# Routed experts in two bf16 halves: weights split during the dense attention, loaded once per expert, picked by a register on TensorE

## The chip, the cores and the metric

One core of a Trainium2 chip runs the whole program. The metric is device time in microseconds (us), the median of the runs shown. TensorE is PE in the profile, its weight loads PEld, VectorE is DVE, ScalarE ACT, GpSimd POOL, and SyncE (which only issues DMAs here) SP.

## The reference

Four layers in a row, each added to `x` (4 x 256 tokens of width 256):

```
x = x + cross_attention(layernorm(x), ctx_2048, ...)   # 16 heads, 4 kv heads, 1601 + 256 keys
x = x + moe(layernorm(x), ...)                         # 32 experts, top 6, plus a shared expert
x = x + window_attention(layernorm(x), ctx_2048, ...)  # 9 keys for each query
x = x + ffn(layernorm(x), ...)                         # weights rounded to e4m3
# moe, for each chosen expert e of a token (H = 256, M = 176):
out = silu(x @ w_gate[e]) * (x @ w_up[e]) @ w_down[e]  # summed over 6 experts with their gates
```

All inputs and the output are float32.

## The kernel before

**The dense attention** (`attend`) takes two thirds of the time. It runs 16 groups (4 batches x 4 kv heads) of 8 tiles of 128 query rows; a tile's turn is a slot, so a job "at (g, i)" is done in slot i of group g. In a slot PE computes the scores of the next tile (L542), turns the probabilities of the last one in four quads (L551) and multiplies them by V in two bf16 halves (L565). ACT copies each turned quad to the high bf16 half (L729) and takes the exponentials (L735); DVE makes the low half (L920) and the row maxima (L907); POOL rotates the keys of the next group. Each engine works through its own list strictly in order.

In some slots an operand in float32 is split into bf16 halves on the side: a job of `JOBS_AT` (L123). SP loads it into one of two `stage` buffers (`split_load`, L337), ACT makes the high half (`split_high`, L757) at a fixed place of its slot, ahead of its third quad copy, DVE makes the low half (`split_low`) at the end of the slot (in slot 6 ahead of the tasks in its middle), and SP stores weights to HBM (`split_store`, L344). Before the change there are 20 jobs: 12 in groups 0 to 2, and context pieces in slots 2 and 6 of groups 5, 6, 9 and 10.

SP's own list orders the DMAs. For each group from 3 on it waits for PE's last output projection of the group before, which runs in slot 1, loads `wo` (L394), stores the rows for the window layer (`near_store`), loads two small tables (L355), and only then comes to the jobs of this group. For job j it first issues the loads up to job j + 1, then the store of j:

```python
for j in [j for j, (at, _) in enumerate(JOBS_AT) if at[0] == g]:
    while ahead < len(SPLITS) and ahead <= j + 1:
        split_load(ahead)
        ahead += 1
    split_store(j)
```

**The experts** (`experts`) come after routing. Tokens are sorted by expert into 80 tiles of 128 rows (NSLOT). There are 96 jobs in one software pipeline: 16 of the shared expert, then 80 routed ones. In step j PE does `gate_up(j)` (L1520), turns the rows of tile j + 2 (`turn_rows`, L1508), does `down(j - 2)` (L1537 and L1538) and turns the hidden values of j - 1 (`turn_hidden`, L1527). All products are float32. ACT does SiLU (L1569), copies the turned rows (L1574) and the result (L1579); DVE multiplies gate and up (L1654) and copies the turned hidden values (L1659). POOL gathers the rows of each tile with an indirect DMA 11 tiles ahead (L1459) and scatters its result with another (L1464). SP loads the weights of each tile's expert (480 and 48 KB, L1433 and L1434) into a ring of eight, with the expert's number read into a register. On the side DVE rounds the last layer's weights to e4m3 (`quantize`, L1686 to L1696): 32 parts of 144 columns, ten operations each, each waiting for the one before, in every second step; and `shares` (L1673 to L1675) takes three operations in each of six steps. After the last scatter SP loads the results back (L1448) and DVE and PE add them to `x`.

Of the kernel before, what the change touches and what calls it, by code (L numbers as in the profile page):

```python
# [15 lines left out]
P = 128  # L16
# [37 lines left out]

FI = 768
# [103 lines left out]
def attend(nc, t, x, groups=GROUPS):  # L159
# [4 lines left out]
    with Scope(nc, "att") as sc:  # L164
# [31 lines left out]
        stage = sc.sb("stage", [P, 2, 1024])  # L196
# [16 lines left out]
        spare = prob[:, :, :]  # L213
        start_from = {("wkv", 0): attn[:, 0:4, :].rearrange("p m d -> p (m d)"), ("wkv", 1): attn[:, 4:8, :].rearrange("p m d -> p (m d)"),
# [12 lines left out]
                 "sums_ready", "mean_done", "mean_ready", "mean_out"]  # L227
# [47 lines left out]
        def split_from(job):  # L275
            kind = job[0]
            return {"wkv": lambda h: t["wkv_l"][:, 512 * h:512 * h + 512], "wq": lambda h: t["wq_l"][:, 1024 * h:1024 * h + 1024],
                    "wo": lambda h: t["wo_l"][:, 1024 * h:1024 * h + 1024],
                    "ctx": lambda b, q: t["ctx_l"][b][:, :, CHUNKS[q][0] * P:(CHUNKS[q][0] + CHUNKS[q][1]) * P]}[kind](*job[1:])

        def staged(job, home):
# [4 lines left out]
            return home[:, 0:512 if job[0] == "wkv" else 1024]  # L286

        def split_to(job, a):

            if job[0] == "ctx":  # L290
                k0, m = CHUNKS[job[2]]
                return kvT[:, job[1] % 2, a, :, S + k0 * P:S + (k0 + m) * P]
            par = job[1] % 2
# [11 lines left out]
        def tokens(b):  # L305

            home = cosd[:, :, :] if b == 0 else flat[:, 1, 0:2 * D].rearrange("p (m d) -> p m d", d=HD)
            return home
# [6 lines left out]
        with nc.Block() as block:  # L315
            @block.sync
            def _(sp):
# [26 lines left out]
                def split_store(j):  # L344
# [3 lines left out]
                    sp.wait_ge(s["split_lo"], j + 1)  # L348
                    dst, src = store_of(job)
# [35 lines left out]
                for g in range(groups):  # L385
# [17 lines left out]
                    if g == 2:  # L403
# [4 lines left out]
                        sp.wait_ge(s["late_stored"], 16 * sum(job[0] != "ctx" and job not in (("wo", 0), ("wo", 1)) for job in SPLITS))  # L408
# [272 lines left out]
            def _(act):  # L681
# [75 lines left out]
                def split_high(j):  # L757
                    job = SPLITS[j]
                    act.wait_ge(stage_in[j % 2], 16 * (j // 2 + 1))
                    if job[0] == "ctx":  # L760

                        wait(act, s["nk_done"], NCH * (job[1] - 1))
                    elif job[0] == "wo":
# [104 lines left out]
            def _(dve):  # L868
# [82 lines left out]
                def normalise(b):  # L951
                    dve.wait_ge(s["rstd_ready"], b + 1)
                    for n in range(2):
# [36 lines left out]
                def extra(i, g):  # L990

                    b, at = g // KVH, (g % KVH, i)
                    if b + 1 < B:
                        if at == STATS_AT:
                            token_stats(b + 1)
                        if at == NORMALISE_AT:
                            normalise(b + 1)
                        for k in TRIG_AT.get(at, ()):
                            trig_step(b + 1, k)
# [1248 lines left out]
```

## Time and profile before

| | us |
|---|---|
| median of 3 runs (1864.81 to 1865.66) | 1865.14 |
| the profiled execution's own time | 1864.89 |
| its span, first to last instruction | 1862.8 |
| PE busy | 1710.4 (92%) |
| DVE, ACT, POOL busy | 1405.2, 1103.7, 1100.0 |

The span's stages: start and first group to 58, full groups of the dense attention to 1183, its last group to 1257, normalisation and routing to 1293, shared expert to 1344, routed experts to 1585, adding up, window attention and last layer to 1863. "Busy" counts an engine's own instructions; the last part of a row, in brackets or behind the bar, is the idle time ahead of the instruction and what ended it.

### The profile page before, as it was taken

Reading aid. Unit: us, or ns where it says so; the run is one execution under the profiler, and the core shown is the slowest. Engines: PE = TensorE matmul, PEld = TensorE weight load, DVE = VectorE, ACT = ScalarE, POOL = GpSimd, SP = SyncE. Lnnn points to the kernel's source line nnn. Section 1 sums busy time; section 2 is a strip of 40 time slices with the busy share of each in tenths; the row PEclk is TensorE's granted clock in tenths of the full one; section 3 lists DMA queues with packets and bytes.
Section 4 is the critical chain, followed back from the end, with each engine's and each line's share of the span. In section 5 each row is a group of like instructions: output and inputs, shape, how many; then the busy total and the mean of one; then the engine's idle time right before and its main releaser. Section 6 shows DMA issues by size and latency. Waiting matters only on the chain. (4 is left out here: it accounts for less than half of the span.)

```text
span 1862.8 us, 41598 instructions
## 1 busy us (share of the span) xinstructions
PE 1710.4 (92%) x14581; PEld 1314.5 (71%) x14727; DVE 1405.2 (75%) x3734; ACT 1103.7 (59%) x2798; POOL 1100.0 (59%) x1718
## 2 busy tenths in 40 slices
PE   4799999999999999999999999986999999589987
PEld 3578777788787787877787887765555555339974
DVE  7898886888877878888788788756656665575746
ACT  6576777676777667777676666652134333173534
POOL 5578695786866958868568577510266664181210
PEclk8899999999999999999999999996999999796998
DMA  3211111011010100110001000325389996500100
GB/s 126 75 52 30 61 39 50 19 36 47 18 39 19 37 20 18 59 32 19 19 19 36 24 1 24 122 92 220 101 253 269 275 267 188 189 15 24 43 9 26
DMA packets 69529, 140.24 MB, mean 75 GB/s; under 512 B 10921, under 2 KB 38674, under 8 KB 69074
## 3 DMA queue, kind: packets, MB, share of 16 engines
q1 hardware_dynamic: 58514, 105.37, 18.3%
q0 software_dynamic: 9984, 30.42, 4.8%
q8 instruction: 120, 1.97, 0.4%
q10 hardware_dynamic: 832, 1.84, 0.3%
q14 instruction: 79, 0.65, 0.1%
HBM read 111.73 MB, written 25.86 MB: 74 GB/s over the span
## 5 line engine op out<-in xcount | busy, mean ns | idle before, releaser
L920 DVE TENSOR_TENSOR att_pT<-att_pT 128x512 bf16<-128x512 f32 (+1 forms) x512 | 320.9, 650 | 166.2 <-ACT att_pT L729 163.1
L565 PE MATMUL att_out<-att_V,att_pT 128*128 128x128 bf16 x5760 | 386.8, 219 | 13.9 <-DVE att_pT L920 12.0
L565 PEld LDWEIGHTS att_out<-att_V,att_pT 128*128 128x128 bf16 x5760 | 349.0, 98 | 40.8 <-DVE att_pT L920 24.3
L729 ACT ACTIVATE att_pT<-att_pT 128x512 bf16<-128x512 f32 (+1 forms) x512 | 278.0, 572 | 128.8 <-PE att_pT L551 128.8
L735 ACT ACTIVATE att_prob<-att_scores,att_negmax 128x512 f32<-128x512 f32 (+1 forms) x512 | 330.3, 655 | 17.5 <-DVE att_negmax L909 16.9
L542 PE MATMUL att_scores<-att_K,att_Q 128*128 128x512 bf16 (+1 forms) x1408 | 298.5, 359 | 7.2 <-DVE att_Q L881 0.5
L907 DVE TENSOR_REDUCE att_mx<-att_scores 128x1 f32<-128x512 f32 (+1 forms) x512 | 291.0, 629 | 1.0 <-PE att_scores L542 0.9
L551 PE MATMUL att_pT<-att_ident,att_prob 128*128 128x128 f32 x1920 | 274.2, 274 | 0.0
L542 PEld LDWEIGHTS att_scores<-att_K,att_Q 128*128 128x128 bf16 x1536 | 150.6, 98 | 144.1 <-issue 1.9
L551 PEld LDWEIGHTS att_pT<-att_ident,att_prob 128*128 128x128 f32 x1920 | 208.6, 141 | 0.8
L465 PE MATMUL att_aux<-att_wkv,att_kvT 128*128 128x256 bf16 x1350 | 167.2, 273 | 17.8 <-DVE att_aT L881 15.2
L653 POOL TENSOR_TENSOR att_scaled<-att_kvraw,att_kw 128x256 f32<-128x256 f32 (+1 forms) x123 | 89.9, 731 | 135.7 <-ACT att_kvraw L697 135.7
L465 PEld LDWEIGHTS att_aux<-att_wkv,att_kvT 128*128 128x128 bf16 x1350 | 127.9, 98 | 35.6 <-DVE att_aT L881 18.8
L655 POOL TENSOR_TENSOR att_cosd<-att_scaled,att_tab 128x256 f32<-128x256 f32 (+2 forms) x153 | 127.2, 831 | 12.0
L1464 POOL DMA_INDIRECT y_s<-moe_ysb,moe_result_row x80 | 79.6, 995 | 76.2 <-ACT moe_ysb L1579 76.2
L667 POOL TENSOR_TENSOR att_rs<-att_rs,att_nhalf 128x2 f32<-128x2 f32 (+2 forms) x153 | 122.5, 801 | 0.0
L1459 POOL DMA_INDIRECT moe_xg<-xrow_s,moe_token_row x80 | 77.8, 972 | 60.4 <-DVE moe_token_row L1643 36.1
L1569 ACT ACTIVATE moe_silu<-moe_up 128x176 f32<-128x176 f32 x96 | 30.5, 318 | 136.0 <-PE moe_up L1520 136.0
L735 ACT ACTIVATION_READ_ACCUMULATOR att_prob<-att_scores,att_negmax 128x1 f32 x512 | 109.5, 214 | 0.0
L1520 PE MATMUL moe_up<-moe_wa,moe_xT 128*128 128x352 f32 x320 | 107.9, 460 | 0.0
L697 ACT ACTIVATE att_kvraw<-att_aux 128x512 f32<-128x512 f32 x120 | 68.7, 572 | 40.4 <-PE att_aux L465 40.1
L662 POOL TENSOR_TENSOR att_rs<-att_kss,att_eps 128x2 f32<-128x2 f32 (+1 forms) x123 | 30.6, 248 | 96.9 <-DVE att_kp L891 96.9
(347 smaller groups left out, 3250.6 us busy)
## 6 DMA issues: line engine op xcount, KB each, us to landing
moe_wa<-in_wa_l SPq DMA_DIRECT2D x80, 480.0 KB
att_wq<-wq_s SPq DMA_DIRECT2D x12, 512.0 KB, 3.7
att_wo<-wo_s SPq DMA_DIRECT2D x12, 512.0 KB, 3.8
att_stage<-in_ctx_l SPq DMA_DIRECT2D x9, 512.0 KB, 4.3
near_s<-att_windows POOLq DMA_DIRECT2D x8, 576.0 KB, 5.5
win_near<-near_s SPq DMA_DIRECT2D x32, 144.0 KB
moe_wb<-in_wb_l SPq DMA_DIRECT2D x80, 48.0 KB
moe_wa<-y_s SPq DMA_DIRECT2D x5, 768.0 KB, 11.0
```

Source lines behind the costliest of these rows:

```text
L465: last = nc.tensor.matmul(o, kvT[:, bp, a, c, k0:k0 + P], wkv[:, par, w, c, :], start=(c, a, w) == (0, 0, 0), stop=(c, a) == (DC - 1, 1))
L542: last = nc.tensor.matmul(scores[:, lo:lo + n], Q[:, u, a, i, :], K[:, u, w, lo:lo + n], start=(a, w) == (0, 0), stop=a == 1)
L551: last = nc.tensor.transpose(pT_ps[j % 2][:, m, :], prob[:, i % 2, k0:k0 + P], ident[:, :])
L565: last = nc.tensor.matmul(out_ps[:, i % 2, :], pT[:, i % 2, a, k, :], V[:, par, k, w, :], start=(k, a, w) == (0, 0, 0), stop=(k, a) == (KT ...
L653: eng.tensor_tensor(a, raw_[:, 0:m, :], weight[:, :].unsqueeze(1).to_broadcast([P, m, HD]), ALU.mult).then_inc(linked, 1)
L655: eng.tensor_tensor(b.rearrange("p m (e f) -> p m e f", e=2), a.rearrange("p m (e f) -> p m e f", e=2), cos.unsqueeze(2).to_broadcast([P, ...
L667: eng.tensor_tensor(scale, scale, nhalf[:, 0:m], ALU.pow).then_inc(linked, 1)
L729: nc.scalar.activation(pT[:, i % 2, 0, 4 * j:4 * j + m, :], pT_ps[j % 2][:, 0:m, :], ACT.Copy).then_inc(s["pt_hi"], 1)
L735: nc.scalar.activation(prob[:, i % 2, lo:lo + n], scores[:, lo:lo + n], ACT.Exp, bias=negmax[:, i % 4:i % 4 + 1], scale=1.0, accum_out=es[ ...
L907: nc.vector.reduce_max(mx[:, i % 2, k:k + 1], scores[:, lo:lo + n], AX.X).then_inc(s["bank_max"], 1)
L920: nc.vector.tensor_tensor(pT[:, i % 2, 1, 4 * j:4 * j + m, :], pT_ps[j % 2][:, 0:m, :], pT[:, i % 2, 0, 4 * j:4 * j + m, :], ALU.subtract) ...
L1520: last = nc.tensor.matmul(up_ps[j % 2][:, 0:GU], rows, w[:, c * GU:(c + 1) * GU], start=c == 0, stop=c == DC - 1)
```

## The change

- The 32 experts' weights are laid out as one array of [32, 128, 1056] float32. 32 more split jobs, `("we", e)`, run in groups 3 to 14 of the dense attention: in slots 0, 2, 6 and 7 of groups 3, 7, 11, 12, 13 and 14, in slots 2 and 6 of groups 4 and 8, in slots 0 and 7 of groups 5 and 9. Both halves go to one buffer in the `windows` tile and from there to HBM by two DMAs; a job's `split_high` waits until the stores of all earlier expert jobs have landed (`expert_out`).
- SP loads the bf16 halves of each expert once, in order of the experts, into a ring of eight, with constant addresses; a place is used again when all tiles of its expert are through. It reports arrivals in order with the semaphore `have`.
- PE reads the tile's expert number into a register, waits for `have`, and addresses the ring with it. Each float32 product becomes three bf16 ones (high x high, high x low, low x high): 6 matmuls of 352 columns for gate and up, 6 of 256 columns for down. The transposes stay float32, and so does the shared expert.
- ACT makes the high half of turned rows and hidden values, DVE the low half from PSUM: two operations on DVE and two on ACT per tile where there was one each.
- `quantize` works on 8 parts of 576 columns and issues one operation in each of the 80 routed steps. `begun_of` (when each expert's tiles begin) is one small DVE operation more. The results come back into `y6` and `w8` (6 places where there were 7).
- `tokens(b)` moves to the other half of `windows`; POOL waits for the expert stores in the last group.

```diff
+SPLIT_E, SPLIT_W = 32, 1056
+EXPERT_AT = [(g, i) for g in range(3, GROUPS - 1) for i in ((0, 2, 6, 7) if g % KVH == 3 or g > 12 or g == 12 else ((2, 6), (0, 7), ())[g % KVH])]
+JOBS_AT = sorted(JOBS_AT + [(at, ("we", e)) for e, at in enumerate(EXPERT_AT)], key=lambda x: x[0])
...
+                    if job[0] == "we":
+                        sp.dma_start(t["wu_s"][job[1]], halves_out[:, :, 0:DC * GU]).then_inc(s["expert_out"], 16)
+                        sp.dma_start(t["wd_s"][job[1]].rearrange("a (p n) -> p a n", p=P), halves_out[:, :, DC * GU:SPLIT_W]).then_inc(s["expert_out"], 16)
+                        return
...
+                    elif job[0] == "we":
+                        wait(act, s["expert_out"], 32 * job[1])
...
-        PARTS = NSLOT * 2 // 5
+        PARTS = NSLOT // QUANT_STEPS
...
+                def fetch(e):
+
+                    u = e % WRING
+                    sp.dma_start(wu[:, u, :, :], t["wu_s"][e]).then_inc(load[u], 16)
+                    sp.dma_start(wd[:, u, :, :], t["wd_s"][e][:, 0:P * D].rearrange("a (p n) -> p a n", p=P)).then_inc(load[u], 16)
+                    sp.dma_start(we[:, u, :, :], t["wd_s"][e][:, P * D:M * D].rearrange("a (p n) -> p a n", p=REST)).then_inc(load[u], 16)
...
+                for e in range(E_ALL):
+                    if e == WRING:
+                        sp.wait_ge(s["begun_of"], 1)
+                    if e >= WRING:
+
+                        begun = sp.value_load(begun_of[0:1, e - WRING + 1:e - WRING + 2], min_val=0, max_val=NSLOT)
+                        sp.wait_ge(s["y_done"], begun + SHARED)
+                    fetch(e)
+                    if e >= BEHIND:
+                        report(e - BEHIND)
...
+                        e = pe.value_load(expert_of[0:1, i:i + 1], min_val=0, max_val=E_ALL - 1)
+                        places[i] = e & (WRING - 1)
+                        first = places[i] * (2 * DC * GU)
+                        pe.wait_ge(s["xt_lo"], i + 1)
+                        pe.wait_ge(s["have"], e + 1)
+                        for c in range(DC):
+                            for a, w in ((0, 0), (0, 1), (1, 0)):
+                                last = nc.tensor.matmul(up, xT[:, i % 3, a, c, :], wu_flat[:, bass.ds(first + (w * DC + c) * GU, GU)],
+                                                        start=(c, a, w) == (0, 0, 0), stop=(c, a) == (DC - 1, 1))
...
+                    first = places.pop(i) * (2 * D)
+                    for c, (w_flat, rows) in enumerate(((wd_flat, P), (we_flat, REST))):
+                        for a, w in ((0, 0), (0, 1), (1, 0)):
+                            last = nc.tensor.matmul(y, hT[0:rows, i % 3, a, c, :], w_flat[:, bass.ds(first + w * D, D)],
+                                                    start=(c, a, w) == (0, 0, 0), stop=(c, a) == (1, 1))
...
+                        dve.wait_ge(s["ht_hi"], i + 1)
+                        V.tensor_tensor(hT[:, i % 3, 1, :, :], ht_ps[j % 2][:, 0:2, :], hT[:, i % 3, 0, :, :], ALU.subtract).then_inc(s["ht_lo"], 1)
```

**How the order moves.** SP in the dense attention, group 12, from its loads of `wkv` to the next group's. Before (`in_...` is an input, `_s` a tensor in HBM that the kernel writes):

```order
L390 DMA att_wkv<-wkv_s 128x1024 [waits att_q_done,att_kv_done]
L391 DMA att_wq<-wq_s 128x2048
L394 DMA att_wo<-wo_s 128x2048 [waits att_wo_done]
L367 DMA ktab_s<-att_raw 65x128 [waits att_nk_ready]
L369 DMA mean_s<-att_mean 1x128 [waits att_mean_ready]
L355 DMA att_ktrig<-in_cosk_l 128x256
L355 DMA att_ktrig<-in_sink_l 128x256
```

and with the change, from its load of `wo` on:

```order
L409 DMA att_wo<-wo_s 128x2048 [waits att_wo_done]
L382 DMA ktab_s<-att_raw 65x128 [waits att_nk_ready]
L384 DMA mean_s<-att_mean 1x128 [waits att_mean_ready]
L370 DMA att_ktrig<-in_cosk_l 128x256
L370 DMA att_ktrig<-in_sink_l 128x256
L353 DMA att_stage<-in_we_l 128x1056 [waits att_split_lo]
L361 DMA wu_s<-att_windows 256x1x704 [waits att_split_lo]
L362 DMA wd_s<-att_windows 128x2x352
```

The load of the job in slot 2 and the two stores of the job in slot 0 stand behind the table loads, and these behind the wait for `wo_done`.

ACT in slot 2 of group 12, before and with the change:

```order
L741 ACTIVATE att_attn<-att_out,att_rinv 128x128 [waits att_rinv_ready,att_pv_done]
L724 ACTIVATE att_V<-att_kvraw 128x2x128 [waits att_kvraw_ready]
L729 ACTIVATE att_pT<-att_pT 128x512 [waits att_pt_done]
L735 ACTIVATE att_prob,att_es<-att_scores,att_negmax 128x512 [waits att_negmax_ready]
L729 ACTIVATE att_pT<-att_pT 128x384 [waits att_pt_done]
```

```order
L756 ACTIVATE att_attn<-att_out,att_rinv 128x128 [waits att_rinv_ready,att_pv_done]
L739 ACTIVATE att_V<-att_kvraw 128x2x128 [waits att_kvraw_ready]
L762 ACTIVATE att_windows<-att_stage 128x1056 [waits att_expert_out,att_stage_in1]
L744 ACTIVATE att_pT<-att_pT 128x512 [waits att_pt_done]
L750 ACTIVATE att_prob,att_es<-att_scores,att_negmax 128x512 [waits att_negmax_ready]
```

The new split copy stands ahead of the third quad copy and of all exponentials of the tile.

PE in one routed step, before and with the change:

```order
L1520 MATMUL moe_up<-moe_wa,moe_xT 128x352 x2
L1508 MATMUL moe_xt<-moe_ident,moe_xg 128x128 x2
L1537 MATMUL moe_y<-moe_wa,moe_hT 128x256
L1538 MATMUL moe_y<-moe_wb,moe_hT 128x256
L1527 MATMUL moe_ht<-moe_ident,moe_h 128x128 x2
```

```order
L1562 MATMUL moe_up<-moe_wu,moe_xT 128x352 x2
L1542 MATMUL moe_xt<-moe_ident,moe_xg 128x128 x2
L1586 ISA
L1586 MATMUL moe_y<-moe_wd,moe_hT 128x256
L1586 ISA
L1586 MATMUL moe_y<-moe_wd,moe_hT 128x256 x2
L1586 REGISTER_ALU
L1586 MATMUL moe_y<-moe_we,moe_hT 128x256
L1586 REGISTER_ALU
L1586 MATMUL moe_y<-moe_we,moe_hT 128x256 x2
L1570 MATMUL moe_ht<-moe_ident,moe_h 128x128 x2
L1555 TENSOR_LOAD moe_expert_of
```

Behind that load follow two ISA rows (L1555), two REGISTER_ALU rows (L1559, L1562), and four more ISA rows among the six matmuls of L1562. So a step has 13 register instructions (one TENSOR_LOAD, eight ISA, four REGISTER_ALU) where it had none, and 16 matmuls where it had 8. An ISA row is a fused group of up to three register operations, or a bound check.

## Rows read from the trace of the kernel before

**Rows 1.** Busy time of routed experts: engine us (instructions) of PE, PEld, DVE, ACT, POOL; clock; DMA share; GB/s

```profile
1344.00:1585.00 241.00, 237.83 (x969) 137.93 (x968) 154.02 (x503) 85.31 (x262) 145.70 (x148) 1.00 0.81 242
```

**Rows 2.** Timeline, PE, routed experts: start, us, engine, line, tiles, count

```profile
1344.37 1.05 PE L1520 MATMUL moe_up<-moe_wa,moe_xT 128*128 128x352 f32 x3
...
1441.95 0.38 PE L1508 MATMUL moe_xt<-moe_ident,moe_xg 128*128 128x128 f32 x2
...
1576.68 1.35 PE L1520 MATMUL moe_up<-moe_wa,moe_xT 128*128 128x352 f32 x4
```

**Rows 3.** Timeline, PE, slot 2 of group 12

```profile
983.78 1.46 PE L477 MATMUL att_aux<-att_wq,att_kvT 128*128 128x512 bf16 x6
985.07 1.34 PE L565 MATMUL att_out<-att_V,att_pT 128*128 128x128 bf16 x21
```

**Rows 4.** Timeline, SP issues, group 12

```profile
978.63 0.32 SPq L394 DMA_DIRECT2D att_wo<-wo_s  x1
...
979.74 0.36 SPq L355 DMA_DIRECT2D att_ktrig<-in_cosk_l  x1
980.14 0.43 SPq L355 DMA_DIRECT2D att_ktrig<-in_sink_l  x1
```

**Rows 5.** Timeline, ACT, slot 2 of group 12 (last: idle before, and what ended it)

```profile
980.29 0.43 ACT L724 ACTIVATE att_V<-att_kvraw 128x256 bf16<-128x256 f32 x1
982.97 0.60 ACT L729 ACTIVATE att_pT<-att_pT 128x512 bf16<-128x512 f32 x1 [2.25 <-PE att_pT L551]
```

**Rows 6.** DMA issues of the whole span: count, KB each, median us to landing

```profile
att_stage<-in_ctx_l SPq DMA_DIRECT2D x9, 512.0 KB, 4.3
...
wo_s<-att_wo SPq DMA_DIRECT2D x4, 512.0 KB, 3.0
```

**Rows 7.** Timeline, slot 0 of group 2: two split jobs back to back

```profile
207.67 2.30 PE L542 MATMUL att_scores<-att_K,att_Q 128*128 128x512 bf16 x11
...
208.70 0.69 ACT L750 ACTIVATE att_kvT<-att_stage 128x512 bf16<-128x512 f32 x1
...
209.28 0.33 SPq L350 DMA_DIRECT2D wo_s<-att_wo  x1
...
211.56 0.60 ACT L729 ACTIVATE att_pT<-att_pT 128x512 bf16<-128x512 f32 x1 [0.52 <-PE att_pT L551]
```

**Rows 8.** Timeline, PE, starts of slots 5 and 7: group 1, then group 4

```profile
180.31 2.30 PE L542 MATMUL att_scores<-att_K,att_Q 128*128 128x512 bf16 x11
...
199.88 0.38 PE L542 MATMUL att_scores<-att_K,att_Q 128*128 128x512 bf16 x1
...
408.33 2.30 PE L542 MATMUL att_scores<-att_K,att_Q 128*128 128x512 bf16 x11
...
426.51 2.30 PE L542 MATMUL att_scores<-att_K,att_Q 128*128 128x512 bf16 x11
```

**Rows 9.** Timeline, SP: three of the first weight loads of the routed experts

```profile
1302.95 0.33 SPq L1433 DMA_DIRECT2D moe_wa<-in_wa_l  x1
1303.46 0.33 SPq L1434 DMA_DIRECT2D moe_wb<-in_wb_l  x1
1304.55 0.33 SPq L1433 DMA_DIRECT2D moe_wa<-in_wa_l  x1
```

**Rows 10.** Timeline, POOL: a scatter and a gather

```profile
1438.13 0.99 POOL L1464 DMA_INDIRECT y_s<-moe_ysb,moe_result_row  x1 [0.56 <-ACT moe_ysb L1579]
1439.42 0.97 POOL L1459 DMA_INDIRECT moe_xg<-xrow_s,moe_token_row  x1 [0.30 <-PE moe_xt L1508]
```

**Rows 11.** DVE groups in 1344 to 1585: count, then busy us, mean ns, idle us before

```profile
L1688 DVE TENSOR_TENSOR moe_y<-moe_w,moe_magic 128x144 f32<-128x144 f32 x32 | 9.9, 308 | 1.1
...
L1674 DVE TENSOR_TENSOR moe_hit<-moe_hit,moe_gates 128x256 f32<-128x256 f32 x6 | 2.5, 424 | 0.2
```

**Rows 12.** Timeline, PE after its idle stretch in the routing

```profile
1290.72 1.03 PE L1480 MATMUL moe_xt<-moe_ones,moe_selb 128*32 128x128 bf16 x8 [4.95 <-POOL moe_ones L1452]
```

**Rows 13.** Busy time of the stretch behind it, columns as in Rows 1

```profile
1291.00:1302.00 11.00, 7.84 (x61) 5.09 (x59) 8.87 (x30) 1.07 (x2) 0.13 (x1) 0.50 0.26 70
```

More of the change, by code:

```diff
@@ L407, in _ @@
                             sp.wait_ge(wo_stored[u], 16)
-                        sp.wait_ge(s["late_stored"], 16 * sum(job[0] != "ctx" and job not in (("wo", 0), ("wo", 1)) for job in SPLITS))
+                        sp.wait_ge(s["late_stored"], 16 * sum(job[0] in ("wkv", "wq", "wo") and job not in (("wo", 0), ("wo", 1)) for job in SPLITS))
                         sp.dma_start(wkv[:, par, :, :, :].rearrange("p a c n -> p (a c n)"), t["wkv_s"][late % KVH]).then_inc(load[par], 16)
@@ L1155 @@
 E_ALL, TOPK, GRP, TOP_GRP = 32, 6, 4, 2
-M = 176
 EXPERTS = E_ALL + 2
-GU = 2 * M
 REST = M - P
 WA = DC * GU + D
+REST_W = M * D // P
+assert SPLIT_E == E_ALL and SPLIT_W == DC * GU + REST_W
 NSLOT = 80
@@ new lines, in quantize @@
+                    w = w8[:, part]
+                    wait(dve, s["quant"], step)
+                    if k == 0:
+                        ins = V.tensor_scalar(magic[:, :].bitcast(I32), w.bitcast(I32), 0x7F800000, None, ALU.bitwise_and)
+                    elif k == 1:
+                        ins = V.tensor_scalar(magic[:, :], magic[:, :], 2.0 ** -6, 1.5 * 2 ** 20, ALU.max, ALU.mult)
+                    elif k == 2:
+                        ins = V.tensor_tensor(y8[:, :], w, magic[:, :], ALU.add)
+                    elif k == 3:
+                        ins = V.tensor_tensor(y8[:, :], y8[:, :], magic[:, :], ALU.subtract)
+                    elif k == 4:
+                        ins = V.tensor_scalar(over[:, :], y8[:, :], E4M3_MAX, 3e38, ALU.is_gt, ALU.mult)
+                    elif k == 5:
+                        ins = V.tensor_scalar(magic[:, :], y8[:, :], -E4M3_MAX, 3e38, ALU.is_lt, ALU.mult)
+                    elif k == 6:
+                        ins = V.tensor_tensor(over[:, :], over[:, :], magic[:, :], ALU.add)
+                    elif k == 7:
+                        ins = V.tensor_scalar(over[:, :], over[:, :], 10.0, None, ALU.mult)
+                    elif k == 8:
+                        ins = V.scalar_tensor_tensor(y8[:, :], y8[:, :], 1.0, over[:, :], ALU.mult, ALU.add)
+                    else:
+                        ins = V.tensor_tensor(wq_flat[:, part], y8[:, :], over[:, :], ALU.subtract)
@@ L1724, in _ @@
                         shares(j - SHARED - 4)
-                    if j >= SHARED + 12 and j % 2 == 0 and part < PARTS:
-                        if part == 0:
-                            dve.wait_ge(s["w8_in"], 16)
-                        quantize(part)
-                        part += 1
-                assert part == PARTS
+                    if j == SHARED:
+                        dve.wait_ge(s["w8_in"], 16)
+                    if SHARED <= j < JOBS:
+                        quantize(j - SHARED)
                 dve.wait_ge(s["share_step"], 3 * TOPK)
```

149 lines of the change are left out of this document (82 added, 67 removed).

## Prediction

> **What bounds the kernel now.** I read the busy time by stage first, then the timelines of PE, then the engines and queues that the change touches. In the routed stage PE is busy 237.8 of 241.0 us at full clock while DMA is at 0.81 [rows 1]: PE bounds, with the weights not far behind. From the first gate-up at 1344.37 to the last at 1576.68 lie 79 steps of (1576.68 - 1344.37) / 79 = 2.941 us, back to back [rows 2]. In the dense attention PE bounds too, but its slack against ACT is small: in slot 2 of group 12 ACT copies its third quad at 982.97 to 983.57 [rows 5], and PE starts the products that need all quads at 985.07 [rows 3]. What delays ACT there by more than about 0.8 us delays PE (1.5 us between the copy's end and the products, of which about 0.7 goes to ACT's next copy and DVE's low half).
>
> The sum is made against the profiled execution, 1864.89 us with a span of 1862.8. It lies 0.25 us below the median of the runs, 1865.14, which I neglect.
>
> **1. Routed steps, from 2.941 to about 2.65 us.** In the trace a bf16 matmul of 512 columns goes by in 1.29 / 6 = 0.215 us (983.78 to 985.07 for six [rows 3]), 0.42 ns a column. By that 6 x 352 columns are 0.89 us, 6 x 256 are 0.65; the four float32 transposes stay, 0.38 for a pair, overlapping, about 0.42 together [rows 2]. The array then works 1.96 to 2.0 us a step. That isn't what sets the step: PE now also reads a register per tile, 13 register instructions in each step, and no register instruction of PE is in the trace of before. The nearest are SP's [rows 9]: from the end of a wb load's issue (1303.79) to the next wa load (1304.55) pass 0.76 us, for one TENSOR_LOAD and three ISA; from wa's end (1303.28) to wb (1303.46) 0.18 us with one ISA, and between two DMAs with no ISA 0.04 (980.10 to 980.14 [rows 4]). So an ISA is 0.14 and the TENSOR_LOAD 0.76 - 0.04 - 3 x 0.14 = 0.30. For PE's sequencer: 0.30 + 8 x 0.14 + 4 REGISTER_ALU at half an ISA (0.28, estimate) + 16 matmuls and 16 weight loads at no more than 0.03 each (0.064 a pair, from 21 pairs in 1.34 us [rows 3]; 0.96) = 2.66. Lower bound: POOL's floor, a scatter of 0.99 and a gather of 0.97 with 0.30 ahead of each, 2.56 us [rows 10] (0.30 is what stands ahead of the gather; the scatter's 0.56 there includes a wait). Upper bound: register work that doesn't hide behind the array at all in its densest part, 0.45 more, 3.1. I take 2.65, nearest to the sum: 79 x (2.65 - 2.94) = -23, and a shorter drain at the end of about 1: **-24** (-31 to +13).
>
> The rule that speaks against the gain: the Trainium skill, page "DMA: Bandwidth & Descriptors", section "Latency and other measured facts", gives a TENSOR_LOAD a floor of about 600 ns. The row disagrees, since the whole gap with it is 0.76 us with three ISA in it; by the page a step would be 0.3 us longer and this term -24 + 24 = 0.
>
> **2. DVE.** `quantize` moves to one operation of 576 columns a step. An operation is 308 ns at 144 columns and 424 ns at 256 [rows 11], 1.04 ns a column, so 0.76 us at 576. DVE's own work is a product of 176 columns (0.34 by the same slope) and two subtractions (0.42 each), 1.9 us with `quantize`: under the step, so hidden. In the six steps with `shares` 3 x 0.42 come on top: 3.2 against 2.65, 6 x 0.5 = **+3**, with `begun_of`'s 0.2 (0 to +5; at a 3.1 us step nothing). ACT's second copies (0.43 each [rows 5]) fit. The weights' DMAs fall from 80 times 528 KB to 32 times 1,056 KB and hide more easily. PE's wait for `have` is for an expert loaded several tiles earlier; I cost it at 0.
>
> **3. Dense attention.** The 32 jobs' instructions lie beside PE. What counts is where ACT, in order, now waits ahead of its exponentials.
>
> *Slot 2.* Eight groups (3, 5, 7, 9, 11 to 14) now have jobs in slots 0 and 2. The load for slot 2 stands in SP's list behind `wo` (issued at 978.63, as PE's last projection ends) and the two table loads, the last of them 980.14 to 980.57 [rows 4]. It can go at 980.57 at the earliest. A load of this kind lands 4.3 us after issue, a store 3.0 [rows 6]: the operand is there at about 984.9 (in groups with an expert in slot 2, the stores of slot 0 at about 984.5 to 986, and `split_high` waits for these too). ACT comes to the copy at 980.72 (980.29 + 0.43 [rows 5]) and its copy takes 1.1 (estimate: 0.43 for 256 columns [rows 5], 0.69 for 512 [rows 7]). It is through at 986.0 to 987.1, where before the third quad copy started at 982.97. Less the 0.8 of slack, PE loses 2.4 to 3.5 us. I take 3.0: 8 x 3.0 = **+24** (from 0, if loads land much faster than the median, to 38).
>
> *Pairs.* (11,7)-(12,0), (12,7)-(13,0) and (13,7)-(14,0): in the pair of group 2, slot 0, the store is issued 1.6 us into the slot (209.28 against 207.67), ACT's turn is at +1.0 (208.70) and its third quad copy at 211.56 [rows 7]. With a store to wait for, landing 3.0 later [rows 6] at 212.3, and a 1.1 us copy, the quad copy goes to about 213.5 : 1.9 each, **+6** (3 to 12).
>
> *Slot 6.* From group 1, with a job in slot 6, slots 5 and 6 take 19.57 us (180.31 to 199.88), from group 4, without one, 18.18 (408.33 to 426.51) [rows 8]: +1.39. Eight expert jobs stand in slot 6: **+11**. In 6 of these groups the job in slot 7 follows a store that lands about 1 us late, 0.3 each after slack, and about ten lone jobs in slots 0 and 7 cost the same by my choice (0 to 0.95, in between): **+5**.
>
> Sum of 3: **+46** (+11 to +66). POOL's wait for the last stores and the moved `tokens` are long past their producers: 0.
>
> **Total:** -24 + 3 + 46 = +25: 1864.9 + 25 = **1890 us**.
>
> **The rivals.**
>
> *(a) The waits cost PE its clock.* After an idle stretch of 4.95 us [rows 12] the granted clock is 0.50, the 1.2 GHz level, for 11 us [rows 13]. The slot-2 waits are about 3 us, shorter, and at 1.00 PE has never stood so long in the attention. If the clock falls in these eight slots, some 1 to 5 us more each: +27, **1917 us**. Chance 0.14. Against it: the waits are shorter and PE is busy on both sides of them.
>
> *(b) Register addressing is dearer on PE than on SP.* The step becomes 3.05, the term 1 becomes +9 and `shares` costs 1: 1864.9 + 9 + 1 + 46 = **1921 us**. Chance 0.14. The Trainium skill, page "TensorE: Matmul & The Clock Gate", section "Wait — 56ns, not 53.3ns?", has a rule that leads here: with hardware decode off the sequencer spends about 62 ns on each matmul, which would add to the register work. The 0.064 us for a pair in the attention speaks neither way, as that pair's array time is about as long.
>
> *(c) The other side: faster.* Mechanism: the load of slot 2 comes early enough. It decides at ACT's delay: if the load and the stores behind `wo` land by 982.5, that is within 2 us of issue, the own copy of 1.1 us ends near the old quad copy's start plus the 0.8 of slack, and slot 2 costs nothing. The medians of 4.3 and 3.0 us speak against it, that both are medians of the busy first groups speaks for it. The attention then costs some 16 (slot 6 and the pairs); with the step at POOL's floor of 2.54 to 2.56 (-31): 1864.9 - 31 + 3 + 16 = **1853 us**. Chance 0.20.
>
> *(d) Both in part,* slot 2 at 1 us each (+8 for 24) with the step at 2.60 (-4): -28 + 3 + 30 = +5, and a little less gives no change. Chance 0.08 within 0.2%.
>
> *(e) The change doesn't do what it says:* the step stays at 2.9 since a chain (transpose, high, low, matmul) and not the work sets it. The attention's price stays, **1911 us**, chance 0.05, within (a) and (b)'s side.
>
> **How the numbers follow.** My forecast (0.39) and (a), (b), (e) (0.33) are slower, (c) faster, (d) between. 0.2% is 3.7 us, about what a measurement of this kernel can tell from no change. Faster 0.2, same 0.08, slower 0.72. The likeliest case's own range is 1872 to 1908, from slot 2 at 1 to 4 us each and the step at 2.55 to 2.75. The range takes in (a), (b) and most of (c): 1851 to 1928.
>
> **What would show it.** Routed step 2.65 us, PE with short idle stretches before its first gate-up matmul and POOL idle a little (a step of 2.55 with POOL back to back is (c), 3.05 is (b)). In groups 12 to 14 slot 2 longer by 2.4 to 3.5 us, ACT idle 3 to 5 us ahead of the expert copy, ended by a DMA; the same in 5 and 9 for the context piece. Slots 5 and 6 together at 19.6 us in groups without a job there before. Granted clock 1.00 throughout the attention; below it, (a). Wrong in kind if slot 2 keeps its length, or if ACT's wait in slots 6 and 7 for the previous stores is longer than in slot 2.

## The result and the profile after

The changed kernel takes 1913.2 us, median of 4 runs (1907.74 to 1916.25), against 1865.4 (1864.81 to 1867.27): 1.0251 times the time before, 95% interval 1.0225 to 1.0277. The forecast was slower, 1890, with a range of 1851 to 1928. All runs compared here had a mean granted clock of 0.946 to 0.963; one run of the last kernel below, 2178 us at 0.737, is left out of its ratio. The profiled execution took 1907.74 us, span 1906.0, 43 us more than the one before; it is the fastest of the four, so its parts fall some 5 us short of the medians' 48. These parts, from the starts of PE's first scores of each slot and of the first gate-up matmul of each routed step:

| | before | after | difference | forecast |
|---|---|---|---|---|
| 8 slots "2" after a job in slot 0 | | | +54.2 | +24 |
| 8 slots "6" | | | +11.4 | +11 |
| 3 pairs across a group's end | | | +3.8 | +6 |
| the rest of the attention | | | +4.7 | +5 |
| attention, to the start of its last slot | | | +74.1 | +46 |
| routing and shared expert | 106.0 | 106.1 | 0 | 0 |
| 79 routed steps | 232.3 | 201.3 | -31.0 | -20 |
| after the last gate-up | 286.1 | 286.1 | 0 | -1 |

The routed forecast is the steps' -23 with the +3 for DVE. So the gain came, larger than forecast, and the loss came where forecast, larger still. Two later kernels keep this attention code unchanged; their eight slots 2 cost 58.0 and 55.7 us where this trace has 54.2, so a difference of under 4 us in that sum says nothing.

**The routed experts.** The busy time of the stage after, answering to [rows 1]:

```profile
1418.00:1622.00 204.00, 193.92 (x1276) 116.40 (x1275) 136.21 (x339) 111.78 (x338) 146.54 (x145) 1.00 0.53 158
```

204 us instead of 241, and the transfers have fallen from 242 to 158 GB/s. Two steps in PE's timeline:

```profile
1502.15 1.07 PE L1562 MATMUL moe_up<-moe_wu,moe_xT 128*128 x6
1503.05 0.38 PE L1542 MATMUL moe_xt<-moe_ident,moe_xg 128*128 128x128 f32 x2
1503.27 0.49 PE L1586 MATMUL moe_y<-moe_wd,moe_hT 128*128 x3
1503.69 0.50 PE L1586 MATMUL moe_y<-moe_we,moe_hT 48*128 x3
1504.12 0.44 PE L1570 MATMUL moe_ht<-moe_ident,moe_h 128*128 128x128 f32 x2
1504.52 1.07 PE L1562 MATMUL moe_up<-moe_wu,moe_xT 128*128 x6
```

This step takes 2.37 us, the one behind it 2.50. Over all, (1619.94 - 1418.65) / 79 = 2.548; eight other kernels below leave the routed code alone, and theirs are 2.52 to 2.57. POOL meanwhile goes from one indirect DMA to the next with nothing but its 0.30 us between them:

```profile
1501.37 0.99 POOL L1498 DMA_INDIRECT y_s<-moe_ysb,moe_result_row  x1 [0.30 <-issue]
1502.66 0.97 POOL L1493 DMA_INDIRECT moe_xg<-xrow_s,moe_token_row  x1 [0.30 <-issue]
```

The median from one scatter to the next is 2.57 us. By these rows POOL sets the step; the prediction had this floor, 2.56, as its lower bound and as the sign of (c).

PE's register instructions, which the trace of before could not show (the number behind the bar of the kind is min / median / max in ns):

```profile
L1555 PEldq TENSOR_LOAD <-moe_expert_of x80: 296/301/756, 1416.9 to 1619.0; - x80
L1555 PEldq FUSED_REGOPS  x80: 151/151/165, 1417.5 to 1619.4; - x80
...
L1562 PEldq FUSED_REGOPS  x320: 46/46/46, 1418.0 to 1620.2; - x160
L1562 PEldq ALU_OP  x80: 36/36/36, 1417.9 to 1619.7; - x80
...
L1586 PEldq FUSED_REGOPS  x160: 46/46/46, 1424.8 to 1625.5; - x160
L1586 PEldq ALU_OP  x160: 32/32/36, 1425.1 to 1625.9; - x160
```

The load takes 0.30 us, exactly what SP's gap gave. But of the eight "ISA" rows of a step, each priced at 0.14 from SP, six take 0.046, one 0.151, and the bound check 0.018. In all a step has 0.30 + 0.15 + 0.02 + 6 x 0.046 + 4 x 0.034 = 0.88 us of it, where the prediction had 1.70.

**The dense attention.** Slot 2 of group 12 went from 9.12 to 17.10 us. SP's issues in it:

```profile
1022.59 0.32 SPq L409 DMA_DIRECT2D att_wo<-wo_s  x1
...
1024.11 0.43 SPq L370 DMA_DIRECT2D att_ktrig<-in_sink_l  x1
1024.58 0.43 SPq L353 DMA_DIRECT2D att_stage<-in_we_l  x1
1025.05 0.53 SPq L361 DMA_DIRECT2D wu_s<-att_windows  x1
1025.62 0.61 SPq L362 DMA_DIRECT2D wd_s<-att_windows  x1
```

The order is the predicted one. ACT, answering to [rows 5]:

```profile
1024.26 0.43 ACT L739 ACTIVATE att_V<-att_kvraw 128x256 bf16<-128x256 f32 x1
1032.38 1.08 ACT L762 ACTIVATE att_windows<-att_stage 128x1056 bf16<-128x1056 f32 x1 [7.70 <-DMA wd_s<-att_windows]
1033.37 0.58 ACT L744 ACTIVATE att_pT<-att_pT 128x512 bf16<-128x512 f32 x1
```

ACT waits 7.7 us for the second store of the job in slot 0. It landed at about 1032.3, 6.7 us after its issue at 1025.62; the medians of the same page are 2.7 and 3.0 us for the two stores. In the six groups with an expert in slot 2 this wait is 6.3 to 7.9 us; in groups 5 and 9 ACT waits 5.5 and 4.8 us for the context load. PE, answering to [rows 3], and the clock behind its wait:

```profile
1027.74 1.46 PE L492 MATMUL att_aux<-att_wq,att_kvT 128*128 128x512 bf16 x6
1034.73 2.42 PE L580 MATMUL att_out<-att_V,att_pT 128*128 128x128 bf16 x21 [5.54 <-DVE att_pT L939]
1036.95 2.72 PE L480 MATMUL att_aux<-att_wkv,att_kvT 128*128 128x256 bf16 x12
```

```profile
1034.70:1039.50 4.80, 4.76 (x33) 4.08 (x34) 2.48 (x7) 2.64 (x8) 3.33 (x5) 0.50 0.16 57
```

The third number from the end is the granted clock: 0.50, the 1.2 GHz level, after 5.54 us of idle. In group 9, whose wait was 2.90 us, it stayed at 1.00, and there the 21 matmuls took 1.59 us (after a wait for DVE, with the quads coming one by one; 1.34 without [rows 3]) and the 12 took 1.48:

```profile
791.70:795.00 3.30, 3.21 (x38) 2.86 (x39) 2.45 (x7) 2.90 (x9) 1.93 (x3) 1.00 0.02 5
```

So the clock costs (2.42 - 1.59) + (2.72 - 1.48) = 2.1 us in group 12. Summed the same way over the eight groups (the query projection too, where PE stopped ahead of it, in groups 3, 7 and 11) it is about 15 us of the 54 (some 14 if the starts of the rows are compared instead of their lengths).

### The profile page after: what moved, and what is told of

Same layout as the page of the kernel before. It is cut to its first block and busy times, and to the rows that moved or that the text cites. A ratio compares the mean times of both kernels' runs of the same rounds, so it can differ in the third digit from the quotient of the medians.

```text
span 1906.0 us, 42659 instructions
## 1 busy us (share of the span) xinstructions
PE 1686.9 (89%) x14901; PEld 1303.1 (68%) x15047; DVE 1426.2 (75%) x3607; ACT 1163.0 (61%) x2910; POOL 1121.0 (59%) x1718
## 5 line engine op out<-in xcount | busy, mean ns | idle before, releaser
L580 PE MATMUL att_out<-att_V,att_pT 128*128 128x128 bf16 x5760 | 394.9, 221 | 39.1 <-DVE att_pT L939 36.9
L580 PEld LDWEIGHTS att_out<-att_V,att_pT 128*128 128x128 bf16 x5760 | 355.2, 99 | 69.6 <-DVE att_pT L939 54.5
L480 PE MATMUL att_aux<-att_wkv,att_kvT 128*128 128x256 bf16 x1350 | 172.0, 278 | 20.3 <-DVE att_aT L900 15.7
L677 POOL TENSOR_TENSOR att_rs<-att_kss,att_eps 128x2 f32<-128x2 f32 (+1 forms) x123 | 36.2, 294 | 137.1 <-DVE att_kp L910 137.1
L679 POOL TENSOR_TENSOR att_cosd<-att_cosd,att_sind 128x128 f32<-128x128 f32 (+2 forms) x153 | 93.7, 612 | 0.0
L1562 PE MATMUL moe_up<-moe_wu,moe_xT 128*128 x480 | 85.4, 314 | 7.8 <-issue 4.8
```

Source lines behind the costliest of these rows:

```text
L480: last = nc.tensor.matmul(o, kvT[:, bp, a, c, k0:k0 + P], wkv[:, par, w, c, :], start=(c, a, w) == (0, 0, 0), stop=(c, a) == (DC - 1, 1))
L580: last = nc.tensor.matmul(out_ps[:, i % 2, :], pT[:, i % 2, a, k, :], V[:, par, k, w, :], start=(k, a, w) == (0, 0, 0), stop=(k, a) == (KT ...
L679: eng.tensor_tensor(b[:, :, 0:HALF], b[:, :, 0:HALF], c[:, :, 0:HALF], ALU.subtract).then_inc(linked, 1)
```

## The experiments

Two theories of slot 2 stood at the start. **Late operands:** load and stores are issued behind `wo_done`, and nothing else is wrong with the jobs. **Own work:** the copy of 1.1 us on ACT and the subtraction on DVE don't fit in slots 2. A third part, contention among the transfers issued together, and a fourth, the clock, were to be priced. The attention's excess over the kernel before is given beside each time, since slots repeat to 0.03 us where nothing waits, but for 0.22 us that some kernels move from one slot to its neighbour.

### Load and stores ahead of the wait

```diff
+                    early = [j for j, (at, _) in enumerate(JOBS_AT) if g >= 3 and at == (g, 0)]
+                    for j in early:
+                        while ahead < len(SPLITS) and ahead <= j + 1:
+                            split_load(ahead)
+                            ahead += 1
+                        split_store(j)
                     if g >= 3 and g + 1 < groups:
                         sp.wait_ge(s["wo_done"], nth("WO", 1, g - 1))
...
-                    for j in [j for j, (at, _) in enumerate(JOBS_AT) if at[0] == g]:
+                    for j in [j for j, (at, _) in enumerate(JOBS_AT) if at[0] == g and j not in early]:
```

> SP alone is changed: from group 3 on, the stores of the job in slot 0 and the load of the next job stand ahead of the wait for wo_done and of the wo and table loads. Late operand theory: they are issued in slot 1 instead of 1.9 to 3.1 us into ACT's slot 2 list, have landed long before ACT's turn, and slot 2 of the eight groups returns to its old length: 54 us less than the changed kernel (attention +20 over the kernel before), about 1854 us. Rival, own work: the copy of 1.1 us on ACT and the subtraction on DVE delay slot 2 whatever the operand does, by 1 to 2 us: 38 to 46 us less, 1862 to 1870. Slots 6 unchanged (+1.43 each) by both.

Measured: 1858.98 us, 0.9948 of the kernel before (0.9929 to 0.9968); attention +21.0, the eight slots 2 together +0.7. ACT has no wait for a DMA in slot 2 of group 12, and PE's products stand at the old length:

```profile
998.40 1.33 PE L586 MATMUL att_out<-att_V,att_pT 128*128 128x128 bf16 x21
999.57 1.47 PE L486 MATMUL att_aux<-att_wkv,att_kvT 128*128 128x256 bf16 x12
```

So the jobs' own work in slot 2 costs nothing, and the whole 54 us hung on where eight loads and stores stand in SP's list. The time is 5 us above the 1854 expected because that was reckoned from the profiled 1907.74; from the median it is 1913.2 - 54 = 1859. That also makes the change a gain, of half a per cent. Timed again beside the last version below:

> The same as e1_jobs_first, timed in more rounds beside b2: 1855 to 1861 us, 0.3 to 0.6% faster than the kernel before.

1858.35 us, 0.9955 (0.9941 to 0.9969).

### Only the load ahead

The same edit without its `split_store(j)` line; the old loop still does the store.

> Only the load for slot 2 goes ahead of the wait for wo_done, the stores of slot 0 stay behind the table loads. If the load's landing is what ACT waits for: as if both were moved, 54 us less. If it is the stores (the releaser that the trace names in six groups, wd_s): groups 5 and 9, whose slot 2 has a context piece that needs no store, lose their 5.7 and 3.4 us, and the other six keep most of their 7.5, less what a 528 KB transfer less beside the stores gives, 1 to 3 us each: 15 to 27 us less in all, 1881 to 1893 us.

Measured: 1877.92 us, 1.0072 (1.0044 to 1.0099); attention +46.8. Groups 5 and 9, which need no store, have lost their excess in slot 2 (5.65 and 3.38 to 0.00). The six others still cost 2.6 to 7.3, together 26.3 where it was 45.1. So both operands are late; the store decides in six groups, where 19 us went with the load (I had expected 6 to 18, and the time came out 3 us below the 1881 to 1893 expected). In group 12 nearly nothing did: its store was issued at 1005.88 and let ACT go at 1012.14, 6.3 us later, so the load ahead of it is not what makes it late there.

### Load and stores behind the wait, ahead of `wo`

As in the first experiment, but `early` stands behind the wait for `wo_done`.

> The load for slot 2 and the stores of slot 0 stay behind the wait for wo_done but go ahead of the wo and table loads. Issue alone: they go 2.0 us earlier, ACT's wait is shorter by that, 8 x 2.0 = 16 us less, 1892. Contention: in the changed kernel the second store lands 6.8 us after its issue, where 3.0 is the median, with wo's 512 KB and the load's 528 KB ahead of it; without wo ahead it lands in 3 to 5 us, at 1028 to 1029 where it was 1032.4, 3.5 to 4.5 us less each in six groups, 3 in the other two: 27 to 33 us less, 1875 to 1881.

Measured: 1870.71 us, 1.0008 (0.9987 to 1.0028); attention +35.4, slots 2 +14.8. ACT's wait in slot 2 of group 11 and the store it waits for:

```profile
926.69 1.08 ACT L768 ACTIVATE att_windows<-att_stage 128x1056 bf16<-128x1056 f32 x1 [3.88 <-DMA wd_s<-att_windows]
```

```profile
921.72 0.61 SPq L362 DMA_DIRECT2D wd_s<-att_windows  x1
```

The store goes 0.32 us into the slot instead of 2.18, and it lets ACT go 5.0 us after its issue; in the changed kernel it was issued at 942.08 and let ACT go at 948.42, 6.3 us. Earlier issue alone was worth 16 by the expectation; the slots 2 gave back 39. The rest is the faster landing without `wo` in front, and the clock, which stays at 1.00 in seven groups (PE idle 1.47 us in group 11, 1.35 in group 12). The run does not part these two, and its time is 4 us below even the 1875 to 1881 expected with both an earlier issue and less contention. In group 14 the clock did fall, after 1.75 us of idle, and that slot costs 3.8 us where groups 12 and 13, with 0.4 us less idle, cost 1.8 and 1.9.

### Matmuls in PE's wait

60 matmuls of 126 columns, one operand zero, added to PE's list in slot 2 of the eight groups. First behind the query projection:

```diff
                     for x_ in amid:
                         task(*x_, g, u)
+                    if i == 2 and (g, 0) in SPLIT_AT and g >= 3:
+                        for _ in range(60):
+                            nc.tensor.matmul(out_ps[:, oi % 2, 0:2 * (KP - NK)], Q[:, u, 0, i, :], prob[:, 0, NK:KP].bitcast(BF16), start=False, stop=False)
                     if old:
                         apply_values(tile, oi, 2, og, opar)
```

> 60 matmuls of 126 columns with a zero operand are added to PE's wait in slot 2 of the eight groups (some 3.4 to 3.8 us of work, the wait is 5.5 us in group 12). Clock theory: PE keeps the clock of 2.4 GHz after the wait, the products behind it take 1.34 and 1.47 us again instead of 2.42 and 2.72: 2.3 us less in each slot, 14 to 18 us less, about 1892. If the lost clock is no part of the price: no change, or up to 4 us more in the groups with a short wait.

Measured: 1920.67 us, 1.0292 (1.0253 to 1.033); slots 2 +63.2. As a total the expectation failed, and the groups say why. In group 12 the matmuls lay in the wait and the excess fell from 7.98 to 5.37:

```profile
1040.73 3.46 PE L613 MATMUL att_out<-att_prob,att_Q 128*128 128x126 bf16 x60
1045.78 1.59 PE L580 MATMUL att_out<-att_V,att_pT 128*128 128x128 bf16 x21 [1.59 <-DVE att_pT L942]
1047.27 1.48 PE L480 MATMUL att_aux<-att_wkv,att_kvT 128*128 128x256 bf16 x12
```

In groups 3, 7 and 11 PE had stopped earlier, ahead of the query projection, since `aux` holds the mean row until ACT copies it, and ACT stands in its wait. There the 60 matmuls came behind the wait, at the low clock, and were plain work:

```profile
957.69 2.74 PE L492 MATMUL att_aux<-att_wq,att_kvT 128*128 128x512 bf16 x6 [5.49 <-ACT att_mean L818]
960.23 4.75 PE L613 MATMUL att_out<-att_prob,att_Q 128*128 128x126 bf16 x60
```

4.75 us for what took 3.46 in group 12. Then with the matmuls ahead of the query projection:

> As e4_dummies, but the 60 matmuls stand ahead of the query projection of slot 2, so that in groups 3, 7 and 11 (where PE first waits there, for the bank that holds the mean row) they too lie in the wait. Clock theory: after e4, where group 12 kept its clock and lost 5.4 us where it was 8.0, while group 11 with the dummies behind the wait rose to 11.7 us from 7.3, now groups 3, 7 and 11 come down as well, to 4 to 6 us: 1889 to 1900 us. Rival, that the dummies are simply work: 3.5 us more where they don't fit, 1913 to 1925.

Measured: 1907.14 us, 1.0224 (1.0205 to 1.0244); slots 2 +43.7, 10.5 less than in the changed kernel, though 28 us of matmuls had been added. Groups 3 and 7 came down to 4.7 and 4.2, as expected; group 11 did not (7.8), where ACT's own wait was 8.4 instead of 7.3 us and PE still stood idle for 2.94. In group 12 the idle rest of 2.18 us was followed by a clock of 0.72 and 2.63 us for the twelve matmuls. Group 13 shows the price of the clock by itself: ACT's wait was 7.60 us, where it was 7.66 in the changed kernel, the clock stayed up, and the slot is 2.5 us shorter (14.82 against 17.31):

```profile
1114.66 1.59 PE L580 MATMUL att_out<-att_V,att_pT 128*128 128x128 bf16 x21 [2.13 <-DVE att_pT L942]
1116.14 1.48 PE L480 MATMUL att_aux<-att_wkv,att_kvT 128*128 128x256 bf16 x12
```

So a part of the price is the clock; but only 10.5 us came back in the slots and 6 in the median (1907 where 1889 to 1900 was expected). The 15 us for all eight groups rest on the sum of rows, not on this run.

### What sets the routed step

Half of the gathers left out, an odd tile reading the rows of the one before:

```diff
-                    wait(pool, s["xt_done"], i - XRING + 1)
+                    wait(pool, s["xt_done"], i - XRING + 2)
+                    if i % 2:
+                        return
...
-                    pe.wait_ge(gathered[i % XRING], 16 * (i // XRING + 1))
+                    i0 = i - i % 2
+                    pe.wait_ge(gathered[i0 % XRING], 16 * (i0 // XRING + 1))
...
```

> Left out: every second gather of rows (an odd tile uses the rows of the tile before). POOL's work per routed step falls from 2 to 1.5 indirect DMAs, 2.57 to 1.93 us. If POOL sets the step of 2.557: it falls to PE's own bound, which by the steps in the changed trace that came early (2.37 us) is 2.3 to 2.4: 79 x 0.17 = 13 us less, about 1900, and POOL shows long idle. If PE's register reading sets it: no change, 1913.

Measured: 1911.8 us; the step is 2.490 instead of 2.548, so 4.6 us in 79 steps and not 13. POOL now waits for ACT's results, 55.8 us between 1430 and 1590 where it was 5.4:

```profile
POOL y_s L1500 <- ACT moe_ysb L1637: 55.8, 31, 18.2
...
PEld moe_up L1565 <- issue: 16.7, 52, 0.6
PEld moe_y L1589 <- issue: 14.6, 67, 0.4
```

So POOL, which sets the step of the changed kernel, stands only some 0.06 us above PE's own bound (0.03 to 0.08, as the same code's step varies between 2.52 and 2.57). Then, in addition, the place in the ring as a constant (the tile's expert is left out of the addressing):

```diff
-                        e = pe.value_load(expert_of[0:1, i:i + 1], min_val=0, max_val=E_ALL - 1)
-                        places[i] = e & (WRING - 1)
+                        e = i * 2 // 5
+                        places[i] = e % WRING
...
-                        begun = sp.value_load(begun_of[0:1, e - WRING + 1:e - WRING + 2], min_val=0, max_val=NSLOT)
-                        sp.wait_ge(s["y_done"], begun + SHARED)
+                        sp.wait_ge(s["y_done"], SHARED + (5 * (e - WRING + 1) + 1) // 2)
```

> As e5_half_gathers, and PE takes the place in the ring from a constant (the tile's expert is left out of the addressing, as if each expert had 2.5 tiles), so it has no register instruction; SP waits on constants too. The difference to e5 prices the register reading and addressing on PE: by my estimate of 2.65 against an array time of 1.96 to 2.0, 0.4 us a step of 2.37, 30 us less than e5; by the durations of the register rows of PE in the changed trace (0.30 + 0.17 + 8 x 0.046 or less, 0.9 in all, partly beside the array) 0.2 to 0.4, 16 to 30 us less. If PE's queue hides them: no difference.

Measured: 1892.82 us, 19 less, of which 16 are the routed steps' (the two profiles' attentions differ by 6 us with the same code); the step is 2.290, and behind the first twelve every step is 2.23 to 2.25, PE without a gap:

```profile
1499.85 1.06 PE L1564 MATMUL moe_up<-moe_wu,moe_xT 128*128 128x352 bf16 x6
1500.74 0.38 PE L1544 MATMUL moe_xt<-moe_ident,moe_xg 128*128 128x128 f32 x2
1500.96 0.49 PE L1588 MATMUL moe_y<-moe_wd,moe_hT 128*128 128x256 bf16 x3
1501.38 0.50 PE L1588 MATMUL moe_y<-moe_we,moe_hT 48*128 48x256 bf16 x3
1501.81 0.44 PE L1572 MATMUL moe_ht<-moe_ident,moe_h 128*128 128x128 f32 x2
1502.09 1.06 PE L1564 MATMUL moe_up<-moe_wu,moe_xT 128*128 128x352 bf16 x6
```

The array's own time is 2.24 us, and from the rows it divides into 0.89 for gate and up, 0.22 and 0.28 for the transposes, and 0.42 and 0.43 for the two halves of down. Reading and using the register adds 2.490 - 2.290 = 0.20 us a step, 16 us in all, with half of the gathers left out. With all of them no run leaves the register out; by POOL's floor the step would then stay near 2.55, so these 16 us are not there to be had by themselves.

### Where a job costs nothing

To see whether the change can be had cheaper, the first experiment's kernel with the jobs in slots 0, 2 and 4:

```diff
-EXPERT_AT = [(g, i) for g in range(3, GROUPS - 1) for i in ((0, 2, 6, 7) if g % KVH == 3 or g > 12 or g == 12 else ((2, 6), (0, 7), ())[g % KVH])]
+EXPERT_AT = [(g, i) for g in range(3, GROUPS - 1) for i in (0, 2, 4) if not (i == 2 and g % KVH in (1, 2) and g < GROUPS - KVH)]
```

> As e1_jobs_first, and the 32 jobs moved to slots 0, 2 and 4 of groups 3 to 14 (not slot 2 where a context piece stands), none in 6 and 7. Against e1 (1859): slot 6 gives back its 8 x 1.43 = 11.4, the jobs in slot 7 their 1.9 and the pairs across the group's end 3 x 1.3 = 4; slot 4 costs 12 times something between 0 (as slots 0 and 2 with early operands) and 1.4 (as slot 6). So 1842 to 1859, by the likelier free slot 1842 to 1846. Faster than the kernel before by more than 1% if slot 4 is free.

Measured: 1860.03 us, 0.9969 (0.9959 to 0.998), just above the upper end of the expectation: attention +22.5. Slots 0 and 2 were free (+0.1 and 0.0) and the pairs' price is gone, but each job in slot 4 costs 1.4 to 2.1 us, which shows in the starts of slots 5 and 6. Then the jobs spread over all slots but 6, never two in a row:

```diff
+EXPERT_SLOTS = {3: (1, 3, 5), 4: (1, 3, 5), 5: (0, 4), 6: (0, 4), 7: (0, 3, 5), 8: (0, 3, 5), 9: (0, 5), 10: (0, 4), 11: (1, 3, 7), 12: (2, 5, 7), 13: (2, 4, 7), 14: (1, 3, 7)}
+EXPERT_AT = [(g, i) for g, slots in EXPERT_SLOTS.items() for i in slots]
```

> As e1_jobs_first, with the 32 jobs spread over slots 0 to 5 and 7 of groups 3 to 14, never in two slots in a row, to read the price of one job in each slot from the starts of PE's slots (slot 0: 0, slot 2: 0, slot 4: 1.4 to 2.0, slot 6: 1.43 are known from e1 and b1). The theory that a job costs PE only what its 1.1 us on ACT exceeds the slot's slack expects each other slot to cost between 0 and 2.0, the same in all groups of one kind; slot 3, whose copy of the near rows stands on ACT too, over 1; slots 1 and 5, with little on ACT ahead of the third quad copy, under 0.5; slot 7 about 1.0, as where e1 shows it. The sum of these is 12 to 25 us above the kernel before's attention, 1855 to 1868.

Measured: 1853.47 us beside 1867.07, one run of each; attention +19.0. Length of whole groups against the kernel before:

| group | jobs in slots | us |
|---|---|---|
| 11 | 1, 3, 7 | -0.23 |
| 14 | 1, 3, 7 | -0.17 |
| 12 | 2, 5, 7 | +1.27 |
| 13 | 2, 4, 7 | +2.09 |
| 7 | 0, 3, 5 | +1.71 |
| 3 | 1, 3, 5 | +1.82 |

In groups 11 and 14 the jobs in slots 1, 3 and 7 are free; my expectation for 3 (over 1), for 5 (under 0.5) and for 7 (1.0) were all wrong. Slot 7 had cost about 1 us in two groups of the first experiment, each time behind a job in slot 6. From this the last version, with SP's order as the change has it:

```diff
+EXPERT_AT = [(g, i) for g in range(3, GROUPS - 1) for i in ((1, 5) if g in (5, 6, 9, 10) else (1, 3, 7))]
...
-    JOBS_AT += [((4 * _b - 3, 2), ("ctx", _b, 0)), ((4 * _b - 3, 6), ("ctx", _b, 1)), ((4 * _b - 2, 2), ("ctx", _b, 2)), ((4 * _b - 2, 6), ("ctx", _b, 3))]
+    JOBS_AT += [((4 * _b - 3, 3), ("ctx", _b, 0)), ((4 * _b - 3, 7), ("ctx", _b, 1)), ((4 * _b - 2, 3), ("ctx", _b, 2)), ((4 * _b - 2, 7), ("ctx", _b, 3))]
```

> The changed kernel with SP's order as it is, but the expert jobs in slots 1, 3 and 7 (in groups 5, 6, 9 and 10 in slots 1 and 5, with the context pieces moved from slots 2 and 6 to 3 and 7), so that no job stands in slot 2, none in two slots in a row, and each operand has a whole slot in hand. By the prices of e8 slots 1, 3 and 7 cost 0 and a job in slot 5 1.3 us: attention 4 to 6 us above the kernel before, where e1 had 21, so about 1843 us, 1840 to 1847: 1.2% faster than the kernel before. If the order on SP is what costs and not the slot, this kernel, with the old order, stays above e1's 1859.

Measured: 1849.99 us, 0.9913 (0.9898 to 0.9929), faster than both kernels; attention +10.4. Groups 11 to 14 are 0.2 us shorter than before with three jobs each. The time is 3 us above the 1840 to 1847 expected. The rest, 4 to 6 us over the expectation, lies in groups 3 to 6, 8, 9 and 10 (0.6 to 2.1 each): in 3, 4 and 8 slots 1, 3 and 7 are not wholly free (0.6 to 0.9 a group), and in 5, 6, 9 and 10 it is the jobs in slot 5 and the moved context pieces, which I did not part. So it isn't SP's order as such that cost, but a job whose operands that order brings late.

## Why the prediction was right, and where it was off

The way and the place of the loss were right, its size was not: +25 us was forecast, and the medians differ by 48. 1913 lies in the range because the range was drawn wide enough for (a) and (b). The sum was also helped by errors of opposite sign: in the profiled execution slots 2 cost 30 us more than forecast, and the routed steps 11 and the pairs 2 less.

**Slot 2, +24 forecast, +54 measured.** The mechanism, the eight groups and the queue were right, and moving those loads and stores takes the whole of it away. The size failed at the step "a load of this kind lands 4.3 us after issue, a store 3.0": these are medians over all such transfers of the run. Here `wo` (512 KB), the tables, the rows, the load (528 KB) and two stores go out within 3.6 us, and in the six groups ACT is let go 5.3 to 6.9 us after the second store's issue. With `wo` behind them instead of ahead it was 5.0 us in group 11; which transfer holds which back is otherwise open. For group 12 I took the operand at 984.5 to 986, 5 to 6.5 us into the slot; it came 8.9 us into it. Less the 15 us for the clock, the waits cost 39 us where I had 24.

**The clock, rival (a).** It came, together with the forecast, not in its place. "The slot-2 waits are about 3 us, shorter" spoke against it, and PE's waits were 2.9 to 5.5 us. In group 9, after 2.90, the clock stayed up; behind 3.59 us (group 5) and more it was down. Its price in (a), 27 us, was too high: after the waits the low clock lasted 2.7 to 5.9 us more, not the 11 of [rows 13].

**Slot 6, pairs, the rest.** 11.4 for 11, 3.8 for 6, 4.7 for 5. The price read from groups 1 and 4, with and without a job in slot 6 [rows 8], carried over to within 0.04 us each. That the rest comes to 5 is in part luck: 1.4 of the 4.7 lies in the last slot of group 2, ahead of all expert jobs, and the two later kernels with the same attention code do not have it.

**Routed steps, 2.65 forecast, 2.548 measured,** 8 us. Two terms were off, in opposite directions. The array takes 2.24 us and not 1.96 to 2.0: the two halves of down take 0.85 instead of 0.65, as 256 columns go by in 0.14 us, near the 0.15 of 352 columns, and the transposes 0.50 instead of 0.42. And PE's register work is 0.9 us instead of 1.70, most of it beside the array. So PE's own bound was 2.490 and not 2.66, and POOL's floor, my lower bound, set the step. Rival (b) fell with it. The rule that led there, 0.062 us of sequencer time for each matmul with hardware decode off (the Trainium skill, page "TensorE: Matmul & The Clock Gate", section "Wait — 56ns, not 53.3ns?"), is not decided by these runs: by it 16 matmuls would take 0.99 us, with the registers 1.87, an estimate from the page's figure, and that hides under the array's 2.24 either way. The floor of 0.6 us for a TENSOR_LOAD (the Trainium skill, page "DMA: Bandwidth & Descriptors", section "Latency and other measured facts") disagrees with PE's rows as it did with SP's: 0.296 to 0.301 us in the ordinary case.

**DVE, +3 forecast.** Steps 7 to 12 are 2.59 to 3.04 us, together 2 us over the 2.5 of the others. The weights' transfers, `have` and POOL's wait for the stores cost nothing visible, as forecast: routing and shared expert took 106.1 us where they took 106.0.

**The other side, (c),** was 1853 us, if the load and the stores behind `wo` land "within 2 us of issue". In the kernel as it is they did not; where I moved their issue, the kernel came to 1858, and with the jobs in other slots to 1850. The price of the other side was within 5 us, and its condition was the one that decides.

## What to carry to other kernels

In slot 2 the work slipped in beside a bound engine cost by when its operands came, not by how long it took. That doesn't hold everywhere: in slots 6 and 4, where ACT never waited for the copy's operand, a job still cost 1.4 and 1.4 to 2.1 us. For each such job, find its load and the store that frees its buffer in the issuing queue's list, and see what waits stand ahead of them. Take the landing time of a transfer from a place where as many others are issued with it, not from the median of the run. And price register instructions from the kind of row they are, not from a gap on another engine: a fused operation took 0.046 us on PE in six cases of seven, and 0.151 in the other, where a gap on SP had suggested 0.14.

## What the runs showed of the hardware

- After idle stretches of PE of 5.5 us (group 12) the granted clock was 0.50 for the next 4.8 us; after 2.90 (group 9) it stayed at 1.00. But in the kernel with load and stores ahead of `wo` it fell after 1.75 us (group 14), and with matmuls put into the wait it fell after 2.18 us (0.72 over the next 3.8 us, group 12 of the second such kernel) and not after 2.13 (group 13), so the length of the idle stretch alone does not say it.
- Matmuls of 256 bf16 columns on this path took 0.14 us each (three in 0.42), those of 352 columns 0.15 (six in 0.89).
- A register read on PE took 0.30 us of its sequencer (once 0.76). Read and addressing together, 13 register instructions, are 0.88 us of sequencer a step, of which 0.20 showed in the step when half of the gathers were left out.
- A store of 352 or 176 KB landed 2.7 or 3.0 us after its issue in the median; behind `wo`, four small transfers and a load of 528 KB it took 4.9 to 5.4 and 5.2 to 6.8.
